# The gate's rows formed per sequence inside the middle pass, with both Newton roots on VectorE

## The chip, the cores and the metric

The kernel runs on one core of a Trainium2 chip. The metric is the device time of one launch in microseconds (us). The engines are TensorE (PE; PEld is its weight load), VectorE (DVE), ScalarE (ACT), GpSimd (POOL) and SyncE (SP), which issues DMAs. Each engine runs its own instructions in order and waits on semaphores for the others.

## The reference

x has 4096 rows of 256 numbers. Six layers are added to it one after the other, each on the layer norm of x: self-attention; an attention over 64 context rows a sequence, with quantised weights; eight pairs of linear maps; a mixture of 8 experts; a masked attention; a quantised feed-forward pair. The change concerns the gate of the fourth layer:

```python
xn = rmsnorm(xf, gate_norm_w, 1e-6)              # xf: layer norm of x, 4096 x 256
xq = act_quant(rmsnorm(xn, gate_in_norm_w, 1e-8))  # per row: round(x * 127 / max|x|) ...
wq = weight_quant(gate_w)                        # 8 x 256, three values
gate_logits = xq @ wq.T
probs = softmax(gate_logits); topw, topi = top_k(probs, 2)
# one expert: its first C = 512 rows of xf (rms-normed), up, silu gate, down, times the row's weight
```

## The kernel before

x stays on the chip as X, 128 partitions by 32 tiles of 256 (four tiles a sequence, eight sequences, besides spare tiles). The stages follow one another, each a block of programs for the five engines: `self_attention`, `middle` (layers 2 and 3), `experts` (layer 4: a block for the gate, the routing and the experts' weights, then a block for the experts), `masked_attention`, `quantised_pair`.

`middle` loops over the sequences, unrolled, with B + 1 iterations. For each sequence TensorE turns the attention weights (`turn_weights`), turns the map's second weights (`turn_w2`, four jobs), computes the next sequence's scores, turns the normalised rows of the sequence before (`f_rows`, L1160), computes `values` (L1209), `outputs` of the sequence before (L1260), `pair` 0 and 1 (L1236: the product of the two maps), `turn_back` (L1273), `rows` of a later sequence and `turn_pair`. The order is written out by hand in each engine's loop, and again in `in_order`, which gives each job one of eight PSUM banks in turn; `take(bank)` waits until the engine that read the bank's last content has released it. ScalarE copies every turned block out of PSUM (L1427 `weights_out`, L1434 `w2_out`, L1411 `f_rows_out`, L1442 `pair_turned`, L1404 `rows_turned_out`, L1454 `wT_turned`, L1461 `outputs_out`) and normalises rows (L1397 `f_normalise`, L1389 `normalise`). VectorE takes the maxima of the scores (L1528), adds the values to X, computes the statistics and the inverse root of the next layer norm (L102 to L135) and adds the outputs (L1564, `add_outputs`), behind which it takes the statistics of the finished rows (L71). GpSimd has eight copies of 8 columns in this stage.

The gate's block begins when `middle` has ended. VectorE aggregates the statistics of all 32 tiles, computes roots by Newton steps (`rsqrt`, L122), forms v = (X - mean) * norm1 and a = v * norm2 in a rolled loop over the sequences (L1985, L1990), takes peaks (L1993), and ScalarE sums the squares of v (L1827). After two more roots VectorE quantises the rows (L2028, L2031), TensorE turns them (L1882), ScalarE copies them (L1834) and TensorE multiplies by the gate's weights (L1888). GpSimd forms u, the rows that the experts get (L1806). From L2041 on VectorE computes the softmax, the two best experts and each row's slot (L2099), after which GpSimd scatters u by slots into the DRAM tensor expert_in, 64 indirect DMAs (L1814); expert_in has first been filled with zeros (L1774). Beside this the experts' weights are loaded (L1783, L1784), summed, rounded to three values and turned.

`masked_attention` handles 32 tiles, four to a sequence; its loops over the first seven sequences are unrolled on GpSimd, TensorE, ScalarE and VectorE (`for b in range(B - 1)`).

Of the kernel before, what the change touches and what calls it, by code (L numbers as in the profile page):

```python
# [1027 lines left out]
def middle(core, context, w_q, b_q, w_k, b_k, w_v, b_v, w_1, b_1, w_2, b_2):  # L1028
# [3 lines left out]
    nc, X, ps, ident = core.nc, core.X, core.ps, core.ident  # L1032
# [4 lines left out]
    BANKS, EARLY = 8, 6  # L1037
    with ExitStack() as ctx:
# [32 lines left out]

        loaded, b_loaded = lasting("loaded"), lasting("b_loaded")
# [15 lines left out]
        early = ["c0", "c1", "cols", "wq", "k0", "k1"] + [f"v{i}" for i in range(B // 2)] + ["wk0", "wk1", "bk"]  # L1088
# [3 lines left out]
        for b in range(B + 1):  # L1092
            if b < B:
                in_order += [("pT", b), ("w2T", b, 0), ("w2T", b, 1)]
            if b + 1 < B:
                in_order += [("scores", b + 1)]
            if b < B:
                in_order += [("w2T", b, 2), ("w2T", b, 3)]
            if b:
                in_order += [("f_rows", b - 1, 0), ("f_rows", b - 1, 1)]  # L1100
            if b < B:
                in_order += [("av", b, 0), ("av", b, 1)]
            if b:
# [3 lines left out]
            if b:  # L1107
                in_order += [("back", b - 1, 0), ("back", b - 1, 1)]
# [4 lines left out]
            if b < B:  # L1113
                in_order += [("wT", b)]
        bank_of = {job: n % BANKS for n, job in enumerate(in_order)}

        with nc.Block() as block:
            @block.sync
            def _(sp):
# [6 lines left out]
                sp.dma_start(bv_row[:], row_of(b_v)).then_inc(loaded, 16)  # L1126
                sp.dma_start(b1_rows[:], b_1.rearrange("g (c p) -> (g c) p", p=P)).then_inc(b_loaded, 16)
# [10 lines left out]
                sp.wait_ge(b_loaded, 16 * 2)  # L1138

            @block.gpsimd  # L1140
            def _(pool):
                pool.wait_ge(cols_out, 1)
                pool.sem_inc(cols_out, -1)
                for g in range(B):
                    if g >= 2:
                        pool.wait_ge(b1_used, 1)
                        pool.sem_inc(b1_used, -1)
                    nc.gpsimd.tensor_copy(w1[:, g % 2, :, D:D + 1], b1_col[:, g * FC:(g + 1) * FC].unsqueeze(2)).then_inc(b1_set, 1)
# [4 lines left out]
            def _(pe):  # L1153
# [122 lines left out]

                for bank in range(BANKS):
                    pe.sem_inc(free[bank], 1)
                pe.wait_ge(loaded, 16 * 9)
                for c in range(DC):  # L1280
                    take(early_bank[f"c{c}"])
                    for t in range(CT):
# [6 lines left out]
                                    ident[0:B * DC, 0:B * DC]).then_inc(cols_full, 1)  # L1289
                over.turn(pe, peak[:])  # L1290
# [38 lines left out]
                last.then_inc(pre_full, 1)  # L1329
                for c in range(DC):  # L1330
# [9 lines left out]
                for b in range(B + 1):  # L1340
                    if b < B:
                        turn_weights(b)
                        turn_w2(b, 0)
                        turn_w2(b, 1)
                    if b + 1 < B:
# [4 lines left out]
                    if b:  # L1350
                        for c in range(DC):
                            f_rows(b - 1, c)
                    if b < B:
                        values(b, 0)
                        values(b, 1)
                    if b:
# [4 lines left out]
                    if b:  # L1361
# [7 lines left out]
                    if b < B:  # L1369
                        turn_pair(b)  # L1370
                for bank in range(BANKS):
# [3 lines left out]
            def _(act):  # L1375
# [87 lines left out]

                act.wait_ge(loaded, 16 * 9)
# [24 lines left out]
                for b in range(B + 1):  # L1489
                    if b < B:  # L1490
                        weights_out(b)
                        w2_out(b, 0)
                        w2_out(b, 1)
                    if b < B:
                        w2_out(b, 2)
                        w2_out(b, 3)
                    if b:
                        for c in range(DC):
                            f_rows_out(b - 1, c)
                    if b + 1 < B:  # L1500
                        powers(b + 1)
                    if b:
# [11 lines left out]
                    if b + 3 < B:  # L1514
                        normalise(b + 3)

            @block.vector
            def _(dve):
# [4 lines left out]
                def less_maximum(bank):  # L1523
# [8 lines left out]
                    dve.drain().then_inc(less_top, 1)  # L1532

# [35 lines left out]

                for b in range(2):  # L1570
# [4 lines left out]
                dve.drain().then_inc(over.ready, 1)  # L1575
# [1709 lines left out]
```

## Time and profile before

| | us |
|---|---|
| median of 3 runs | 2373.59 (2372.21 to 2380.17) |
| the profiled execution's own time | 2368.86 |
| its span, first to last instruction | 2367.1 |
| mean granted TensorE clock | 0.853 of full speed |
| busy: TensorE / VectorE / ScalarE / GpSimd | 1715.8 / 1550.3 / 1394.6 / 788.3 |

Times of instructions are counted from the start of the span. Busy time leaves out waits, register and semaphore instructions. The stages begin, by their first instructions, at about 1097.8 (middle), 1370.3 (gate, routing and weights), 1609.8 (experts), 1823.0 (masked attention) and 2196 us (quantised pair). A number in brackets behind an instruction is the time for which its engine was idle before it, with what ended that.

### The profile page before, as it was taken

The numbers are of one execution on the slowest core, as the hardware profiler recorded it, in microseconds if no ns is written. First come the engines' busy times: TensorE is split into PE (matmuls) and PEld (weight loads), VectorE is DVE, ScalarE is ACT, GpSimd is POOL, SyncE is SP. The second block draws the span as 40 slices with busy tenths as digits, with TensorE's granted clock in tenths as the row PEclk, the third lists the DMA queues.
The fourth block names the chain that finished last, engine by engine and source line by source line (L and its number), as shares of the span: only waits on it lengthen the run. The fifth ranks groups of instructions, "written<-read, shape, count | busy, mean of one in ns | idle before, by whom it ended". The sixth has DMA issues, their size and how long they took to land. (4 is left out here: it accounts for less than half of the span.)

```text
span 2367.1 us, 42843 instructions
## 1 busy us (share of the span) xinstructions
PE 1715.8 (72%) x13321; PEld 1084.2 (46%) x13338; DVE 1550.3 (65%) x3111; ACT 1394.6 (59%) x2215; POOL 788.3 (33%) x749
## 2 busy tenths in 40 slices
PE   3789998989999898985888802122443788888577
PEld 1455555555555555553666601121222355555323
DVE  6877777777777777775233386744774675755775
ACT  3889888898979898991444412443553332323745
POOL 0534545454545455450000050470001444443000
PEclk9999999999999999996789955555766787878699
DMA  5222222222222222222122111332102201111001
GB/s 180 61 53 62 59 55 64 61 53 62 62 50 64 59 64 53 64 46 97 36 72 72 36 76 53 122 109 89 54 27 70 81 25 30 23 32 18 1 10 63
DMA packets 173822, 140.04 MB, mean 59 GB/s; under 512 B 83794, under 2 KB 155399, under 8 KB 173366
## 3 DMA queue, kind: packets, MB, share of 16 engines
q1 hardware_dynamic: 166710, 122.78, 19.4%
q0 software_dynamic: 6912, 14.71, 2.7%
q8 instruction: 111, 1.82, 0.3%
q14 instruction: 89, 0.73, 0.1%
HBM read 61.92 MB, written 20.97 MB: 35 GB/s over the span
## 5 line engine op out<-in xcount | busy, mean ns | idle before, releaser
L577 ACT ACTIVATE a_p_hi<-ps,a_probs_up,a_s_scale 128x512 f16<-128x512 f32 x512 | 397.7, 777 | 54.9 <-ACTq L575 54.1
L689 DVE TENSOR_REDUCE a_top<-ps 128x2 f32<-128x1024 f32 x256 | 313.1, 1223 | 132.6 <-DVEq L688 132.6
L578 ACT ACTIVATE a_probs<-ps,a_probs_up,a_s_scale 128x512 f32<-128x512 f32 x512 | 398.5, 778 | 0.0
L917 POOL TENSOR_TENSOR a_p_lo<-a_probs,a_p_hi 128x1024 f16<-128x1024 f32 x128 | 277.8, 2170 | 210.4 <-POOLq L916 169.1
L905 POOL TENSOR_TENSOR a_ops<-a_ident_down,a_top 64x256 f16<-64x256 f32 x256 | 158.9, 621 | 340.8 <-POOLq L900 332.3
L698 DVE TENSOR_TENSOR a_p_lo<-a_probs,a_p_hi 128x1024 f16<-128x1024 f32 x128 | 182.7, 1427 | 41.2 <-DVEq L697 41.2
L441 PE MATMUL ps<-a_ops 128*128 128x512 f16 x512 | 195.8, 382 | 17.7 <-PEq L439 17.6
L460 PE MATMUL ps<-a_v_hi,a_p_hi 128*128 128x65 f16 x2048 | 205.6, 197 | 2.1 <-PEq L455 2.0
L463 PE MATMUL ps<-a_v_lo,a_p_hi 128*128 128x64 f16 x2048 | 205.6, 195 | 0.0
L464 PE MATMUL ps<-a_v_hi,a_p_lo 128*128 128x65 f16 x2048 | 205.5, 196 | 0.0
L460 PEld LDWEIGHTS ps<-a_v_hi,a_p_hi 128*128 128x128 f16 x2048 | 191.2, 99 | 23.0 <-issue 11.1
L463 PEld LDWEIGHTS ps<-a_v_lo,a_p_hi 128*128 128x128 f16 x2048 | 190.6, 100 | 13.1 <-issue 1.4
L442 PE MATMUL ps<-a_ops 128*128 128x512 f16 x512 | 196.0, 383 | 0.0
L464 PEld LDWEIGHTS ps<-a_v_hi,a_p_lo 128*128 128x128 f16 x2048 | 190.6, 99 | 0.0
L427 PE MATMUL ps<-a_qk,a_qd 128*128 128x512 f16 x512 | 152.7, 380 | 46.1 <-PEq L425 45.9
L414 PE MATMUL ps<-a_wp,a_oT 128*128 128x256 f32 x512 | 128.7, 396 | 1.1 <-PEq L370 1.1
L2498 POOL TENSOR_TENSOR x_s<-x_s,x_top 128x1024 f32<-128x1024 f32 x32 | 60.8, 1899 | 156.2 <-POOLq L2497 106.4
L1814 POOL DMA_INDIRECT expert_in<-g_u,m_slot x64 | 79.2, 1237 | 100.9 <-POOLq L1811 81.7
L671 DVE SCALAR_TENSOR_TENSOR a_qk<-ps,a_qk 128x512 f16<-128x512 f32 x128 | 88.5, 691 | 34.9 <-DVEq L670 34.9
L385 PE MATMUL ps<-a_xnT,a_wq 128*128 128x512 f16 x384 | 94.5, 382 | 20.7 <-PEq L370 20.7
L414 PEld LDWEIGHTS ps<-a_wp,a_oT 128*128 128x128 f32 x512 | 94.8, 195 | 12.2 <-issue 1.3
L427 PEld LDWEIGHTS ps<-a_qk,a_qd 128*128 128x128 f16 x512 | 46.0, 97 | 117.1 <-issue 82.7
(487 smaller groups left out, 3767.3 us busy)
## 6 DMA issues: line engine op xcount, KB each, us to landing
a_ops<-a_qk SPq DMA_DIRECT2D x384, 128.0 KB, 2.3
f_w<-in_L_ffn_W_dram SPq DMA_DIRECT2D x16, 1024.0 KB, 7.6
a_qd<-a_qk SPq DMA_DIRECT2D x128, 64.0 KB, 2.2
g_a<-in_L_attn_gp_w_dram SPq DMA_DIRECT2D x8, 1024.0 KB
X<-in_x_dram SPq DMA_DIRECT2D x8, 512.0 KB, 9.9
expert_in<-g_w SPq DMA_DIRECT2D x8, 512.0 KB
g_a<-in_L_attn_dp_w_dram SPq DMA_DIRECT2D x8, 512.0 KB
e_x_in<-expert_in SPq DMA_DIRECT2D x8, 512.0 KB, 4.3
```

The lines of the kernel that those rows point to most:

```text
L414: last = nc.tensor.matmul(ps[:, JOB + bank, 0:D], oT[:, c, t * P:(t + 1) * P], wp[:, c, :], start=(c % (HC // 2) == 0), stop=(c % (HC // 2 ...
L427: last = nc.tensor.matmul(ps[:, ROW + j % 2, :], qd[:, s, j, :], qk[:, s, K_HI, :], start=True, stop=True)
L441: nc.tensor.matmul(ps[:, st_bank(n), :], ops[:, s, i, A_K, keys], ops[:, s, i, A_Q, :], start=True, stop=False)
L442: nc.tensor.matmul(ps[:, st_bank(n), :], ops[:, s, i, B_K, keys], ops[:, s, i, B_Q, :], start=False, stop=True).then_inc(st_full, 1)
L460: first = nc.tensor.matmul(ps[:, AV, at:at + HD + 1], hi, v_hi[:, k, h, :], start=(k == 0), stop=False)
L463: nc.tensor.matmul(ps[:, AV, at:at + HD], hi, v_lo[:, k, h, :], start=False, stop=False)
L464: last = nc.tensor.matmul(ps[:, AV, at:at + HD + 1], lo, v_hi[:, k, h, :], start=False, stop=(k == KT - 1))
L577: nc.scalar.activation(p_hi[:, h % 2, k, :], scores, ACT.Exp, bias=probs_up[:], scale=s_scale[:])
L578: nc.scalar.activation(probs[:, h % 2, k, :], scores, ACT.Exp, bias=probs_up[:], scale=s_scale[:]).then_inc(st_taken, 1)
L689: nc.vector.tensor_reduce(top[:, c % 2, 2 * pair:2 * pair + 2], ps[:, ROW:ROW + 2, :], AX.X, ALU.max).then_inc(row_taken, 1)
L698: nc.vector.tensor_tensor(p_lo[:, h % 2, 0:2, :], probs[:, h % 2, 0:2, :], p_hi[:, h % 2, 0:2, :], ALU.subtract).then_inc(p_made, 1)
L917: nc.gpsimd.tensor_tensor(p_lo[:, h % 2, 2:KT, :], probs[:, h % 2, 2:KT, :], p_hi[:, h % 2, 2:KT, :], ALU.subtract).then_inc(p_made_pool, 1)
```

## The change

The gate's block keeps only what follows L2041. All that stood before is moved into `middle`: its loop gets B + GATE_STEPS = 13 iterations instead of B + 1 = 9, and a sequence's gate is worked on in five steps, each an iteration behind the other. `f_rows` moves ahead of `scores` on TensorE and `f_rows_out` ahead of two of the `w2_out` on ScalarE. u is formed by ScalarE instead of GpSimd, and ScalarE instead of VectorE does the rounding. The buffers `gate.u` and `gate.logits` live from `middle` to the experts; `a` has three slots of one sequence. The experts' weights no longer wait for the gate (`w_used` is given at once). In `masked_attention` the four unrolled loops become loops of the engines with b in a register.

The diff, cut to its core:

```diff
-        for b in range(B + 1):
+        for b in range(B + GATE_STEPS):          # in_order, and on TensorE, ScalarE, VectorE
             if b < B:
                 in_order += [("pT", b), ("w2T", b, 0), ("w2T", b, 1)]
+            if 1 <= b <= B:
+                in_order += [("f_rows", b - 1, 0), ("f_rows", b - 1, 1)]
+            if 0 <= b - GATES < B:
+                in_order += [("gates", b - GATES)]
             if b + 1 < B:
                 in_order += [("scores", b + 1)]
...
+            if 0 <= b - QUANTISE < B:
+                in_order += [("gate_rows", b - QUANTISE)]
+    NORMS, ROWS, SQUARES, QUANTISE, GATES = 1, 2, 3, 4, 5
...
+                sp.dma_start(gw[:], gate_w).then_inc(gate_loaded, 16)
+                sp.dma_start(norm1[:], row_of(gate_norm)).then_inc(gate_loaded, 16)
+                sp.dma_start(norm2[:], row_of(gate_in_norm)).then_inc(gate_loaded, 16)
...
+                def gate_rows(b):      # TensorE, last in an iteration
+                    for t in range(TT):
+                        for c in range(DC):
+                            last = nc.tensor.transpose(ps16(bank)[:, at:at + P], g_r[:, t, c * P:(c + 1) * P], ident16[:])
+                def gates(b):          # TensorE, between f_rows and scores
+                    for t in range(TT):
+                        for c in range(DC):
+                            last = nc.tensor.matmul(ps[:, bank, t * E:(t + 1) * E], g_rT[:, t, c, :], gwT[:, c, :], ...)
...
+                def experts_rows(b):   # ScalarE
+                    act.wait_ge(u_ready, 1)
+                    for t in range(TT):
+                        nc.scalar.activation(gate.u[:, n, :], X[:, n, :], ACT.Identity, scale=u_factor[:, t:t + 1], bias=u_shift[:, t:t + 1])
+                    act.wait_ge(v_made, 1)
+                    for t in range(TT):
+                        nc.scalar.activation(g_junk[:, t * D:(t + 1) * D], g_v[:, t, :], ACT.Square, accum_out=squares[:, t:t + 1])
+                    act.drain().then_inc(squared, 1)
+                def quantise(b):       # ScalarE
+                    act.wait_ge(per_made, 1)
+                    for t in range(TT):
+                        nc.scalar.activation(a[:, t, :], a[:, t, :], ACT.Identity, scale=per[:, b % 2, t:t + 1], bias=up[:])
+                    act.drain()
+                    nc.scalar.activation(g_r, a, ACT.Identity, bias=minus_up[:])
+                def gate_rows_out(b):  # ScalarE: 128 x 1024 bf16 out of PSUM
...
                     if b < B:
                         pair_turned(b, 0)
+                    if 0 <= b - QUANTISE < B:
+                        quantise(b - QUANTISE)
+                    if b < B:
                         pair_turned(b, 1)
...
                     if b + 3 < B:
                         normalise(b + 3)
+                    if 0 <= b - QUANTISE < B:
+                        gate_rows_out(b - QUANTISE)
+                    if 0 <= b - ROWS < B:
+                        experts_rows(b - ROWS)
...
+                def gate_norms(b):     # VectorE: 4 bn_aggr, 3 small, 2 paired, seed (2 paired + 1), 3 Newton steps of 3
+                def gate_values(b):    # 2 paired, 1 small -> u_ready; v: 4 rows -> v_made; a: 128 x 1024; peaks
+                def gate_squares(b):   # wait squared; 3 small, seed, 3 Newton steps of 3
+                def gate_steps(b):     # 6 small -> per_made
+                def gate_logits(b):    # wait gates_full; 1 small, releases the bank
...
                     if b < B:
                         add_values(b)
                         f_statistics(b)
-                    if b:
+                    if 0 <= b - GATES < B:
+                        gate_logits(b - GATES)
+                    if 0 <= b - SQUARES < B:
+                        gate_squares(b - SQUARES)
+                    if 0 <= b - ROWS < B:
+                        gate_values(b - ROWS)
+                    if 1 <= b <= B:
                         add_outputs(b - 1)
+                    if 0 <= b - NORMS < B:
+                        gate_norms(b - NORMS)
+                    if 0 <= b - SQUARES < B:
+                        gate_steps(b - SQUARES)
```

In `experts`, on VectorE (TensorE, ScalarE and GpSimd lose their parts of the gate in the same way), and in `masked_attention`:

```diff
                     nc.vector.memset(zeros, 0.0).then_inc(zeros_made, 1)
                     nc.vector.memset(ones_col[:], 1.0)
                     nc.vector.memset(ones[:], 1.0)
-                    row_moments(core, dve)
-                    ...                       # L1943 to L2039: roots, v, a, peaks, quantised rows, logits
+                    dve.sem_inc(w_used, 2)
+                    dve.wait_ge(made, 1)
+                    dve.sem_inc(made, -1)
+                    nc.vector.tensor_copy(number[:], counting[:])
+                    dve.drain()
+                    nc.vector.tensor_scalar(base[:], number[:], float(ROOM), -float(ROWS), ALU.mult, ALU.add)
                     nc.vector.tensor_reduce(top[:], logits[:], AX.X, ALU.max)
...
-                for b in range(B - 1):
+                with pool.Fori(0, B - 1) as b:      # the same on TensorE, ScalarE and VectorE
```

## Rows read from the trace of the kernel before

**Rows 1.** Busy by stage: stretch, length, PE, PEld, DVE, ACT, POOL (instructions), clock, DMA share, GB/s.
```profile
1097.80:1370.30 272.50, 221.83 (x1028) 164.28 (x1028) 98.75 (x375) 114.23 (x266) 1.51 (x8) 0.85 0.20 68
1370.30:1483.30 113.00, 15.79 (x132) 11.71 (x132) 84.14 (x199) 21.85 (x72) 34.67 (x21) 0.50 0.19 68
```
**Rows 2.** Timeline of the gate's block and its end: start, us, engine, instruction, idle before.
```profile
1370.59 0.91 DVE L1938 MEMSET g_w<- 128x1024 f32 x1 [0.55 <-PEq L1117]
...
1483.25 0.42 DVE L2041 TENSOR_REDUCE g_top<-g_logits 128x32 f32<-128x256 f32 x1
...
1503.27 0.16 DVE L2097 TENSOR_SCALAR m_slot<-m_share 128x8 uint32<-128x8 f32 x1
...
1504.56 1.53 POOL L1814 DMA_INDIRECT expert_in<-g_u,m_slot  x1 [81.70 <-POOLq L1811]
...
1609.86 0.06 DVE L2388 MEMSET e_minus_round<- 128x1 f32 x1 [34.67 <-PEq L1766]
```
**Rows 3.** Timeline of one sequence of the middle pass, ScalarE and TensorE.
```profile
1225.76 0.38 ACT L1442 ACTIVATE f_both<-ps 128x256 f32<-128x256 f32 x1 [3.82 <-ACTq L1441]
...
1231.20 2.08 ACT L1389 ACTIVATE c_xn<-X,c_shift,c_ln_rstd 128x256 f32<-128x256 f32 x4
...
1233.47 0.59 ACT L1427 ACTIVATE c_probsT<-ps 64x512 f32<-64x512 f32 x1 [0.19 <-ACTq L1426]
...
1238.23 0.60 ACT L1411 ACTIVATE f_xnT<-ps 128x512 f32<-128x512 f32 x1 [0.20 <-ACTq L1410]
...
1239.40 5.97 PE L1260 MATMUL ps<-f_xnT,f_wT 128*128 128x512 f32 x8 [3.05 <-PEq L1156]
...
1249.57 3.65 PE L1236 MATMUL ps<-f_w,f_w2T 128*128 128x257 f32 x16
...
1253.34 0.38 ACT L1442 ACTIVATE f_both<-ps 128x256 f32<-128x256 f32 x1 [3.82 <-ACTq L1441]
```
**Rows 4.** Busy time and clock of two stretches of the same sequence.
```profile
1233.47:1245.37 11.90, 8.56 (x23) 4.50 (x22) 5.90 (x27) 5.92 (x16) 0.00 (x0) 0.71 0.04 11
1245.37:1253.10 7.73, 7.73 (x42) 6.74 (x41) 2.69 (x6) 1.22 (x3) 0.00 (x0) 1.00 0.00 0
```
**Rows 5.** The line L1427, once a sequence: durations in ns, first and last start.
```profile
L1427 ACT ACTIVATE c_probsT<-ps x8: 590/590/590, 1151.6 to 1336.6; 64x512 f32<-64x512 f32 x8
```
**Rows 6.** Busy time and DMA share behind the start of the gate's block.
```profile
1380.00:1390.00 10.00, 0.35 (x2) 0.28 (x2) 8.58 (x22) 0.66 (x3) 5.94 (x3) 0.50 0.37 147
```
**Rows 7.** Prices of operations like the moved ones: timeline, and one line.
```profile
1240.21 0.16 DVE L131 TENSOR_TENSOR f_ln_tmp<-f_ln_rstd 128x4 f32<-128x4 f32 x1
...
1240.44 0.16 DVE L133 TENSOR_TENSOR f_ln_tmp<-f_ln_tmp,f_ln_half 128x4 f32<-128x4 f32 x1
...
1426.65 1.66 DVE L1985 SCALAR_TENSOR_TENSOR g_v<-X,mean_var,g_norm 128x256 f32<-128x256 f32 x4
...
1428.51 1.23 DVE L1990 TENSOR_TENSOR g_a<-g_v,g_norm 128x1024 f32 x1 [0.20 <-issue]
...
1486.68 1.06 ACT L1844 ACTIVATE g_junk<-g_a 128x1024 bf16<-128x1024 f32 x1
...
L1827 ACT ACTIVATE g_junk<-g_v x32: 398/401/417, 1389.3 to 1438.5; 128x256 bf16<-128x256 f32 x32
```
**Rows 8.** VectorE's last work in the middle pass.
```profile
1368.64 1.41 DVE L71 BATCH_NORM_STATS2 row_stats<-X 128x6 f32<-128x256 f32 x4
```
**Rows 9.** Transposes with and without register addresses, and a loop's branch on TensorE.
```profile
1463.46 1.21 PE L1882 MATMUL ps<-ident,g_r 128*128 128x128 bf16 x8 [0.57 <-PEq L1878]
...
1510.70 1.86 PE L1911 MATMUL ps<-ident,g_w 128*128 128x128 bf16 x16 [12.92 <-PEq L1908]
...
L2330 PEldq COMPARE_BRANCH  x6: 83/215/215, 1669.2 to 1783.4; - x6
```
**Rows 10.** Masked attention from the first to the last tile's turned weights, 31 tiles.
```profile
1883.60:2188.60 305.00, 251.25 (x1157) 174.27 (x1156) 193.57 (x413) 90.09 (x121) 136.85 (x107) 0.81 0.15 28
```

More of the change, by code:

```diff
@@ L1289, in _ @@
                                     ident[0:B * DC, 0:B * DC]).then_inc(cols_full, 1)
+                pe.wait_ge(gw_part, 1)
+                pe.sem_inc(gw_part, -1)
+                take(early_bank["gw"])
+                nc.tensor.matmul(ps[:, early_bank["gw"], 0:1], ones[:], gw_sum[:], start=True, stop=True).then_inc(gw_total, 1)
                 over.turn(pe, peak[:])
@@ L1329, in _ @@
                 last.then_inc(pre_full, 1)
+                pe.wait_ge(gw_round, 1)
+                pe.sem_inc(gw_round, -1)
+                take(early_bank["gwT"])
+                for c in range(DC):
+                    last = nc.tensor.transpose(ps[:, early_bank["gwT"], c * E:(c + 1) * E], gw[:, c * P:(c + 1) * P], ident[0:E, 0:E])
+                last.then_inc(gw_turned, 1)
                 for c in range(DC):
@@ L1338, in _ @@
                 pe.sem_inc(v_made, -1)
-                for b in range(B + 1):
+                for b in range(B + GATE_STEPS):
                     if b < B:
@@ L1344, in _ @@
                         turn_w2(b, 1)
+                    if 1 <= b <= B:
+                        for c in range(DC):
+                            f_rows(b - 1, c)
+                    if 0 <= b - GATES < B:
+                        gates(b - GATES)
                     if b + 1 < B:
@@ L1488, in _ @@
                 normalise(2)
-                for b in range(B + 1):
+                for b in range(B + GATE_STEPS):
                     if b < B:
@@ L1493, in _ @@
                         w2_out(b, 1)
+                    if 1 <= b <= B:
+                        for c in range(DC):
+                            f_rows_out(b - 1, c)
                     if b < B:
@@ L1496, in _ @@
                         w2_out(b, 3)
[L1497 to L1499 removed]
                     if b + 1 < B:
                         powers(b + 1)
[L1502 removed]
+                    if 1 <= b <= B:
                         for m in range(DC):
@@ new lines, in gate_logits @@
+                def gate_logits(b):
+                    bank, seq = bank_of["gates", b], slice(b * TT, (b + 1) * TT)
+                    dve.wait_ge(gates_full, 1)
+                    dve.sem_inc(gates_full, -1)
+                    nc.vector.scalar_tensor_tensor(out=gate.logits[:, seq, :], in0=ps[:, bank, 0:TT * E].rearrange("p (t e) -> p t e", e=E),
+                                                   scalar=gw_mean[:], in1=g_step[:, seq].unsqueeze(2).broadcast_to([P, TT, E]),
+                                                   op0=ALU.mult, op1=ALU.mult).then_inc(free[bank], 1)
@@ L1568, in add_outputs @@
                         row_statistics(core, b * TT + t)
+                nc.vector.memset(ones[:], 1.0)
+                nc.vector.memset(gw_sum[:], 0.0)
+                nc.vector.memset(up[:], ROUND)
+                nc.vector.memset(minus_up[:], -ROUND)
                 for b in range(2):
@@ L2653, in _ @@
                 ahead.turn(pe)
-                for b in range(B - 1):
+                with pe.Fori(0, B - 1) as b:
                     sequence(b, more=True)
@@ L2718, in _ @@
                 power(0)
-                for b in range(B - 1):
+                with act.Fori(0, B - 1) as b:
                     sequence(more=True)
@@ L2808, in _ @@
                 maximum(0, 1)
-                for b in range(B - 1):
+                with dve.Fori(0, B - 1) as b:
                     sequence(b, more=True)
```

350 lines of the change are left out of this document (167 added, 183 removed).

## The prediction

> **What bounds the kernel now.** I read the busy time by stage first. The stage from 1370.30 to 1483.30 us, the gate, is the one that the change takes out: 113.0 us in which VectorE is busy 84.14, ScalarE 21.85 and TensorE 15.79 [rows 1]. It is a serial chain. It ends when VectorE takes the row maxima of the logits (L2041) at 1483.25 [rows 2]; everything that the change keeps begins there. From L2041 to the last slot is 20.3 us, then GpSimd, idle for 81.70 us before it, scatters for 105 us, and the next block starts at 1609.9 [rows 2]. The expert weights, rounded beside the scatter, do not set that end: VectorE, which rounds them, has been idle for 34.67 us when it comes [rows 2]. So a us taken out ahead of L2041 is a us of the whole, as long as the filling of the inbox with zeros, the other thing that the scatter waits for, stays ahead.
>
> The second view is one sequence of the middle pass, in order of time. The work that the gate is moved into is not slack. From the copy of one sequence's second pair product (L1442, 1225.76) to TensorE's outputs (L1260, 1239.40) ScalarE works without a gap: it copies, normalises (L1389 and its like), copies again (L1427, L1434, L1411), and L1260 waits 3.05 us for the last of these copies [rows 3]. After that wait the granted clock is low: 0.71 over the stretch with L1260, 1.00 over the one behind it [rows 4]. So ScalarE's burst, 13.6 us, and TensorE's stretch from L1260 to the end of L1236, 13.8 us, add up with the hand-overs to the local period, 27.6 us from one L1442 to the next; the mean period, by L1427, is 185.0/7 = 26.4 us [rows 5]. VectorE is busy only 98.75 of the stage's 272.5 us [rows 1].
>
> **Part 1: the gate's stage goes.** Ahead of L2041 there remain the memset of zeros, two small ones, the wait for GpSimd's constants and two copies of 8 columns: from 1370.59 about 2.0 us instead of 112.7 [rows 2]. That is -110.6 us. GpSimd's own u rows ended long before the scatter and save nothing by themselves. Bounds: -111 (nothing in the way) to -104. The latter is the inbox: its zeros are written until the window 1380 to 1390 (DMA share 0.37) and were started at about 1371.6, so they land some 13 us after the stage begins [rows 6]; slots are now made at 2.0 + 20.3 = 22.3 us, 9 us later. The first two experts' weights are now queued right behind the zeros, and their load may lengthen that; I leave 7 us for it in the range and nothing in the sum.
>
> **Part 2: what a sequence's gate costs VectorE.** A small operation with its drain starts every 0.24 us (1240.21 to 1240.44) [rows 7]. `gate_norms`, `gate_squares`, `gate_steps` and `gate_logits` have 15 + 14 + 6 + 1 such steps, 8.7 us, and the aggregates and paired operations 0.6. `gate_values` has three small ones, four rows in 1.66, a 1024-wide product of 1.23 and a maximum of the same length: 5.0 us [rows 7]. Together 14.4 us a sequence, both roots being here; with the 98.75/8 = 12.3 us of now VectorE is busy some 27 of a period of 30 at the worst. It stays behind TensorE only by its order: `f_normed` comes ahead of the new work, `less_maximum` comes 10 us after it. I cost this at nothing in the steady state. If the cover fails, the bank of `gates` (released by VectorE's `gate_logits`) is the one that `pair` 0 takes, 8 banks later: VectorE releases it about 5.8 us after `values`, about when L1260 ends.
>
> **Part 3: what it costs ScalarE, which is on the path.** `experts_rows` stands at the end of an iteration, ahead of the next `weights_out`: four scaled rows as in L1389, 2.08 us, and four squares at 0.40 us with their drain, 1.9; `gate_rows_out` reads 1024 columns, 1.06 by the nearest row, 1.25 with its drain [rows 3, 7]. `quantise` (2.08 + 1.06 + drains = 3.4 us) stands between the two pair products' copies, where ScalarE waits 3.82 us anyway [rows 3]: nothing. In the other direction the new order puts `f_rows_out` ahead of two `w2_out`, so that L1260 need not wait for these: 2 x 0.80 = -1.6 us. By sequence: iteration 1: -1.6; iterations 2 and 3: +4.0 - 1.6 = +2.4 each; iterations 4 to 7: +5.2 - 1.6 = +3.6 each. Sum +17.6. TensorE's own additions (eight transposes of 128 columns, eight products of 8) are some 1.3 us a sequence and lie in the time that it waits for ScalarE; that wait grows to some 7 us, and with it the chance that more of L1260 and the pair product behind it run at the low clock: at most 2 us a sequence, of which I take 0.7, or +5. Steady state: +23, between +5 (ScalarE's additions half hidden) and +40 (the bank of part 2 and the clock both in full).
>
> **Part 4: head and tail of the middle pass.** Head: three loads, two small TensorE jobs, and the rounding of the gate's weights ahead of four batches of statistics: +1.4 us, 0 to 3. Tail: four more iterations, in which nothing covers the chain of sequence 7. From the end of its statistics, 1368.64 + 1.41 = 1370.05 [rows 8]: norms 4.2, steps of sequence 5 1.5, logits and squares of 6 3.8, values of 7 5.0, steps of 6 1.5, logits and squares of 7 3.8, steps of 7 1.5: 21.3. `quantise` of 7 is done at 25.6 (ScalarE is first held by sequence 6 until 22.3), the transposes at 27.1, the copy at 28.4, the products at 29.3, the logits at 29.7. +30 us, 26 to 36.
>
> **Part 5: the masked attention's loop.** The diff also rolls it up on four engines. What was a constant becomes a register. Eight transposes with a register address take 1.21 us, sixteen without one 1.86: 151 against 116 ns, +35 ns each [rows 9]. TensorE has ten such products a tile, VectorE's two or three lie behind waits at perhaps 0.1 us together: 0.45 x 28 tiles = 12.6. A TensorE loop branch takes 0.215 us [rows 9], seven of them 1.5. Upper end 14, lower end 0 if all is hidden in the 9.8 us that a tile takes (305.0/31) [rows 10]; TensorE and waits for it make most of a tile, so I take rather more than half, +8. The Trainium skill ("Advanced Engine Details and Errata", Control Flow Timing) gives a compare-and-branch about 108 ns. By it the seven would be 0.8 us instead of 1.5; the row is twice that on TensorE.
>
> **Sum:** -110.6 + 23 + 1.4 + 30 + 8 = -48 us. The profiled execution took 2368.86 us (span 2367.1); the median of the three runs is 2373.59, 4.7 above. -48 from the median gives 2325, from the profiled one 2321. I say 2324.
>
> **The rivals.**
> A: *the middle pass absorbs it.* ScalarE's new work meets gaps after all and the rolled loop is free: steady +8, loop 0, giving -71: 2303. For it: TensorE is the busiest engine there (221.83 of 272.5) [rows 1] and ScalarE less than half busy. Against: the burst ahead of L1260 has no gap [rows 3]. Chance 0.2.
> B: *VectorE becomes the bound of the middle pass.* The two roots hold `add_outputs` or the gates' bank, and each of seven periods grows by 4 us more: -20, 2354. For it: 27 busy us with in-order waits in a period of 30. Against: by my order of events each release comes 0 to 2 us ahead of its use. Chance 0.2.
> C: *slower: the jump back of the rolled loop.* If each jump has to fetch its code anew, the seven jumps of the slowest engine stand on the path. It decides from (48 + 7)/7 = 7.9 us a jump. Against it: the branches of the expert loops, six on TensorE, show 0.215 us [rows 9]; the gain of part 1 is there anyway. At 9 us a jump it would be -48 + 63 = +15: 2389. Chance 0.04. The Trainium skill ("Advanced Engine Details and Errata", ISA Cache) says that the instruction cache has two lines of 256 instructions, more on TensorE. By this rule only a body above 512 instructions would fetch on each turn, and no row here counts a body.
> D: *the stage does not shrink as said:* the scatter is held by the zeros or the weights queued behind them by over 30 us, with the middle pass lengthened all the same: about 2360 to 2373. Chance 0.03.
> My forecast: 0.53.
>
> **How the numbers follow.** Forecast's own range is 2310 to 2338 (loop 0 to 14, tail and steady state by half their bounds). To hold 8 in 10 it has to reach over most of A and of B: 2299 to 2353. 0.3% is 7 us, about what this kernel's runs (2372.21 to 2380.17) can tell from no change. Faster: the forecast, A, B and half of D, with a little taken off for what I have not seen: 0.94. Within 0.3%: 0.02. Slower: 0.04.
>
> **What would show it.** In the changed profile: the block of the experts' weights should last about 129 us from its first memset to the next block instead of 239; GpSimd's scatter should begin 23 us after it; the middle pass should last about 327 us instead of 272.5, 30 of them behind sequence 7's statistics; the distance of L1427's successors should be under 27 us in the first sequences and about 30 from the fifth on, with L1260's successor waiting for ScalarE's copies and not for VectorE; a tile of masked attention should take 10.1 us instead of 9.8. The prediction is wrong if less_maximum or add_outputs is late in the middle pass (B), if the first matmul behind a jump waits (C), or if the scatter starts later than 25 us (D).

## The result, and the profile after

The changed kernel takes 2303.27 us, the median of four runs (2302.21 to 2308.77), beside 2372.9 us of the kernel before: ratio 0.9715, 95% interval 0.9674 to 0.9757, so 58 to 77 us less. Measured once more, on the chip of the first experiments, it took 2306.23 us beside 2370.48, ratio 0.9726 (0.9701 to 0.9751), so 64 us less. The prediction was 2324, 49 us less; the time lies in its range, and it is faster as said. But the number is that of rival A (2303), and neither of A's two reasons holds: the middle pass did not absorb the gate, and the rolled loop was not free, it gave 16.9 us. And 2303 lies outside the forecast's own range, 2310 to 2338; only the wider range, which was stretched over A, holds it.

First the stages of the changed kernel, from the profiled execution (2308.77 us, span 2307.0). The stretches are the middle pass, the block of the experts' weights, the middle pass from the first to the last weights_out (L1508, seven periods), and masked attention from its first to its last tile (31 tiles); the columns are as in [rows 1].

```profile
1102.10:1437.20 335.10, 247.85 (x1160) 182.27 (x1160) 188.57 (x803) 177.60 (x410) 1.83 (x11) 0.78 0.17 56
1437.20:1567.30 130.10, 25.97 (x210) 23.51 (x210) 67.04 (x205) 49.02 (x57) 81.87 (x66) 0.55 0.47 162
1158.50:1366.80 208.30, 179.87 (x871) 137.56 (x870) 117.96 (x497) 118.58 (x288) 1.21 (x6) 0.85 0.18 61
1839.30:2127.10 287.80, 225.16 (x1157) 157.86 (x1156) 193.16 (x413) 90.12 (x121) 138.25 (x108) 0.89 0.16 29
```

The same two stretches of the kernel before, the seven periods and the 31 tiles:

```profile
1151.60:1336.60 185.00, 165.33 (x817) 127.56 (x817) 63.54 (x240) 87.47 (x211) 1.18 (x6) 0.88 0.21 69
1882.50:2187.20 304.70, 251.96 (x1157) 174.44 (x1156) 193.40 (x413) 89.93 (x121) 137.78 (x107) 0.80 0.15 28
```

The middle pass grew from 272.8 to 335.1 us (+62.3), the experts' first block shrank from 239.3 to 130.1 (-109.2), and the masked attention's tiles, which the gate never touches, shrank from 304.7 to 287.8 (-16.9). The self-attention ahead of it all, which the change does not touch, ended 4.3 us later (in a second profile of the changed kernel 2.1 us earlier, so this is spread). These four make -59.5 of the -60.1 between the two spans; the medians lie 69.6 us apart, and the other 9.5 us are spread between runs that no profile splits up. In the last row TensorE executes the same 1157 products as before, but is busy 27 us less, at a clock of 0.89 instead of 0.80. That is the surprise.

The end of the middle pass and the scatter answer to [rows 2] and [rows 8], from the timeline:

```profile
1405.42 1.41 DVE L71 BATCH_NORM_STATS2 row_stats<-X 128x6 f32<-128x256 f32 x4
...
1434.83 0.36 PE L1341 MATMUL ps<-gate_gwT,gate_rT 128*128 128x8 bf16 x8 [1.48 <-PEq L1202]
1435.35 0.25 DVE L1743 SCALAR_TENSOR_TENSOR gate_logits<-ps,gate_gw_mean,gate_step 128x32 f32<-128x32 f32 x1 [5.73 <-DVEq L1742]
...
1437.16 0.91 DVE L2114 MEMSET g_w<- 128x1024 f32 x1 [1.56 <-PEq L1159]
...
1438.44 0.41 DVE L2123 TENSOR_REDUCE g_top<-gate_logits 128x32 f32<-128x256 f32 x1
...
1459.75 1.24 POOL L2030 DMA_INDIRECT expert_in<-gate_u,m_slot  x1 [21.97 <-issue]
```

From the end of sequence 7's statistics (1406.83) to the next block's memset there are 30.3 us, before 0.5: the tail costs 29.8, and 30 was said. The scatter starts 22.6 us into the block (23 was said), and the block lasts 130.1 us (129 was said).

### The profile page after: what moved, and what is told of

Its sections match the earlier page's. It is cut to its first block and busy times, and to the rows that moved or that the text cites. A ratio compares the mean times of both kernels' runs of the same rounds, so it can differ in the third digit from the quotient of the medians.

```text
span 2307.0 us, 43352 instructions
## 1 busy us (share of the span) xinstructions
PE 1705.8 (74%) x13321; PEld 1076.1 (47%) x13338; DVE 1558.2 (68%) x3345; ACT 1437.8 (62%) x2287; POOL 756.4 (33%) x732
## 5 line engine op out<-in xcount | busy, mean ns | idle before, releaser
L441 PE MATMUL ps<-a_ops 128*128 128x512 f16 x512 | 197.8, 386 | 17.8 <-PEq L439 17.7
L460 PEld LDWEIGHTS ps<-a_v_hi,a_p_hi 128*128 128x128 f16 x2048 | 191.8, 100 | 23.3 <-issue 12.0
L385 PE MATMUL ps<-a_xnT,a_wq 128*128 128x512 f16 x384 | 94.5, 382 | 20.6 <-PEq L370 20.6
L385 PE MATMUL ps<-a_xnT,a_wk 128*128 128x512 f16 x384 | 93.9, 381 | 5.5 <-PEq L370 5.4
```

The source lines that it names most:

```text
L385: last = nc.tensor.matmul(ps[:, JOB + bank, :], w[:, i, d, c * P:(c + 1) * P], xnT[:, j, d, :], start=(n == d == 0), stop=(n == len(PARTS) ...
L441: nc.tensor.matmul(ps[:, st_bank(n), :], ops[:, s, i, A_K, keys], ops[:, s, i, A_Q, :], start=True, stop=False)
L460: first = nc.tensor.matmul(ps[:, AV, at:at + HD + 1], hi, v_hi[:, k, h, :], start=(k == 0), stop=False)
```

## The experiments

Four questions: is it the loop that shortens masked attention, by which engine, and how; does VectorE or ScalarE set the middle pass's period; what is the new order worth; and can the middle pass be had cheaper. "The 31 tiles" and "seven periods" are the two stretches above. Eleven changed kernels and the changed kernel itself were run.

**The loop alone, on the kernel before.**

```
-                for b in range(B - 1):
+                with pe.Fori(0, B - 1) as b:      # and so for pool, act, dve
```

> The kernel before with only the masked attention's loop over the sequences rolled up on its four engines; nothing else of the change. It prices part 5 alone. The masked attention took 288.2 us for 31 tiles in the changed kernel instead of 305.0, at a granted clock of 0.90 instead of 0.81. Theory R (the roll itself does it): 288 us for 31 tiles here too (9.3 us a tile), the whole 15 to 17 us shorter than before. Rival L (what stands ahead of it does it: the gate's stage is gone, the code or the tiles lie elsewhere, or it differs from run to run): 300 to 315 us for 31 tiles, and by my own prices (35 ns for each TensorE product with a register address, 0.215 us a branch) the whole 0 to 14 us longer.

Measured: ratio to before 0.9938 (0.9915 to 0.9962), 2354.39 us beside 2370.48. The 31 tiles took 288.2 us at a clock of 0.89, and seven periods of the middle pass 183.2, as before. The loop alone gives the gain of the masked attention. Theory R holds; my price for it had the wrong sign.

**The mirror: the changed kernel with the loop written out.**

> The changed kernel with the masked attention's loop written out again on all four engines; the gate stays in the middle pass. Theory R (the roll gives the 17 us): 305 us for 31 tiles at a clock near 0.81, and the whole 15 to 17 us longer than the changed kernel, about 2318 to 2320 us beside its 2303. Rival L (the move of the gate gives it): 288 us for 31 tiles at 0.90, the whole within 5 us of the changed kernel. My prediction's price (rolled is 8 us dearer) would make it 8 us shorter than the changed kernel, about 2295.

Measured: 2314.95 us beside 2306.23 of the changed kernel on the same chip; ratio to before 0.9767 (0.9734 to 0.9801). The 31 tiles took 293.9 us, between the two. The single tiles, read from one x_pT (ScalarE's copy of a tile's turned attention weights) to the next, show why: of the seven sequences one ran at the full clock throughout its long tile (12.9 us), two fell once (17.3), the other four as in the kernel before (19.3 to 19.7). Not all of the 12.9 is the clock: in that tile VectorE makes x_o (the tile's output, for which TensorE waits) 1.3 us behind x_pT, in the others 2.9 to 3.5 us behind it, and the tile two places ahead of it took 11.6 us at a clock of 0.85 instead of 9.97. Written out, the same code falls into one pattern or the other; its runs spread over 20 us (2305.58 to 2325.85), those of the rolled kernel over 7.

**The changed kernel once more.**

> The changed kernel itself once more, on the same chip as the others, so that they can be set against it, and a second profile of it. If the 288.2 us for 31 tiles of masked attention belong to the kernel, they stand within 2 us again; if they vary by chance with the clock, they may be anywhere from 288 to 305.

Measured: 2306.23 us, ratio 0.9726 (0.9701 to 0.9751). The 31 tiles took 288.0 us, so they belong to the kernel (from the sixth tile to the thirtieth it is 225.6 and 225.9 us in the two profiles of the changed kernel and 245.5 in that of the kernel before; the first tiles vary by some us whatever is changed). The seven periods took 214.2 us and not 208.3:

```profile
1150.40:1364.60 214.20, 185.93 (x871) 141.34 (x870) 117.97 (x497) 118.57 (x288) 1.20 (x6) 0.82 0.18 60
```

The difference lies in the first two periods (26.3 and 32.0 us instead of 28.2 and 24.1); the other five agree within 0.2. Three other profiles with this order show the second form (214.2, 214.1, 214.1), so it is the usual one, and I go by it below.

**TensorE's loop rolled alone; then the other three without it; then VectorE's alone.** All on the kernel before, with the one line above.

> The kernel before with the masked attention's loop rolled up on TensorE alone. So far: unrolled, the 31 tiles took 304.7 us (all four engines written out, before) and 293.8 (written out, in the changed kernel), rolled on all four 287.8 to 288.2 in three profiles. A sequence's long fourth tile shows why: rolled, the granted clock falls once in it (17.3 us, and 4.33 for the next tile); unrolled it falls a second time behind a short wait of TensorE (19.3 us, and 5.9). Theory P (it is TensorE's own instruction order and timing in its loop that keep the second fall away): 288 us here. Theory O (it is when the other engines deliver): 300 to 305 us. A loop on TensorE alone should show in any case tiles at the full clock of 10.11 and 5.85 us instead of 9.97 and 5.67, if the register addresses cost what I gave them.

> The mirror of the run with TensorE alone: the kernel before with the loop rolled up on ScalarE, VectorE and GpSimd, TensorE's written out. Theory P: 300 to 305 us for the 31 tiles, tiles at the full clock of 9.97 and 5.67 us. Theory O: 288 us.

> The kernel before with the masked attention's loop rolled up on VectorE alone. Rolled on ScalarE, VectorE and GpSimd it gave 284.2 us for the 31 tiles, on TensorE alone 300.1, on none 304.7. If it is VectorE (its register addresses move when it frees the scores and hands over x_o): 284 to 290 us and the whole about 15 us shorter, with one tile of each sequence at 10.11 us instead of 9.97. If it is GpSimd or ScalarE: 300 to 305 us and the whole unchanged.

Measured: TensorE alone 1.0005 (0.9994 to 1.0016), the 31 tiles 300.1 us. The other three 0.9941 (0.9923 to 0.9959), 284.2 us. VectorE alone 0.9921 (0.9896 to 0.9947), 288.4 us. So VectorE's loop is enough, and TensorE's does not do it. Theory P, TensorE's own order, falls; theory O holds. No run rolls ScalarE's or GpSimd's loop alone, or all but VectorE's. The forms are not clean everywhere: with TensorE's loop alone two of the seven long tiles (17.1 us) fall once as well, and with the other three rolled three of seven take 14.7 us, each with a tile of 11.6 us two places ahead of it; with VectorE's alone one of seven does.

What happens is seen in single tiles. Four tiles of one sequence, from x_pT to x_pT, in the kernel before; then in the changed one; then with VectorE's loop alone; then with TensorE's alone. The long tile is the first row of each:

```profile
1986.40:2005.60 19.20, 13.25 (x49) 9.49 (x50) 10.18 (x18) 3.80 (x6) 10.66 (x9) 0.63 0.32 51
2005.60:2011.60 6.00, 5.86 (x28) 3.60 (x27) 2.51 (x3) 1.98 (x3) 0.00 (x0) 0.75 0.14 16
2011.60:2021.90 10.30, 9.20 (x44) 6.07 (x44) 9.29 (x19) 3.83 (x5) 3.91 (x3) 1.00 0.00 1
2021.90:2027.60 5.70, 5.53 (x33) 4.16 (x32) 4.54 (x20) 2.27 (x4) 3.90 (x4) 1.00 0.03 7
```

```profile
1943.40:1960.80 17.40, 10.34 (x49) 7.26 (x50) 10.27 (x18) 3.83 (x6) 10.35 (x9) 0.80 0.25 43
1960.80:1965.10 4.30, 4.23 (x28) 3.04 (x26) 2.30 (x2) 1.97 (x2) 0.50 (x1) 1.00 0.63 69
1965.10:1975.20 10.10, 9.14 (x44) 6.09 (x44) 9.10 (x18) 3.84 (x5) 3.14 (x2) 1.00 0.00 0
1975.20:1981.10 5.90, 5.63 (x34) 4.17 (x32) 4.80 (x21) 2.24 (x3) 4.14 (x4) 1.00 0.00 0
```

```profile
1958.10:1975.50 17.40, 10.61 (x49) 7.43 (x50) 10.28 (x18) 3.82 (x7) 10.33 (x9) 0.80 0.19 45
1975.50:1979.80 4.30, 4.18 (x28) 3.10 (x26) 2.35 (x2) 1.95 (x2) 0.50 (x1) 1.00 0.42 66
```

```profile
1984.40:2004.00 19.60, 13.27 (x49) 9.55 (x50) 10.10 (x18) 3.84 (x7) 10.60 (x9) 0.63 0.29 50
2004.00:2009.70 5.70, 5.56 (x28) 3.53 (x26) 2.51 (x3) 1.98 (x3) 0.00 (x0) 0.78 0.12 11
```

The same 49 products take 13.3 us in one and 10.3 in the other, because of the clock. Finer stretches of the long tile, before and after:

```profile
1988.00:1994.00 6.00, 4.11 (x7) 2.07 (x8) 4.03 (x9) 1.33 (x2) 3.91 (x3) 0.51 0.25 44
1995.00:1998.00 3.00, 2.57 (x22) 2.29 (x20) 2.56 (x6) 0.30 (x1) 1.16 (x1) 1.00 0.12 18
1999.00:2008.00 9.00, 7.41 (x21) 4.62 (x20) 0.85 (x2) 2.84 (x4) 3.91 (x4) 0.50 0.42 58
```

```profile
1945.00:1951.00 6.00, 3.75 (x6) 1.82 (x7) 4.38 (x9) 1.34 (x2) 3.92 (x3) 0.50 0.21 41
1952.00:1955.00 3.00, 2.48 (x22) 2.21 (x20) 2.82 (x5) 0.40 (x1) 0.69 (x1) 1.00 0.21 26
1955.00:1964.00 9.00, 6.31 (x39) 4.68 (x40) 2.53 (x5) 3.04 (x5) 5.23 (x5) 1.00 0.43 56
```

In both the clock falls to half (1.2 of 2.4 GHz) within TensorE's wait for x_o (3.65 us before, 3.90 after), and comes back. In the kernel before it falls a second time, between the second and the third of these rows, and stays low for all 9 us of the third; in the changed one TensorE has gaps there too (6.31 of 9 us busy), and the clock stays. The sequence saves 19.2 + 6.0 - 17.4 - 4.3 = 3.5 us, and six such make 21. The first sequence does not have it (26.2 us instead of 24.1 for these two tiles), and the rest of the difference to 16.9 is the price of the addresses and of the first tiles. The register addresses do cost something, and it can be read where both run at the full clock: from one x_pT to the next 9.97 us becomes 10.11 with VectorE rolled, 5.67 becomes 5.85 with TensorE rolled. That is 0.32 us a sequence in these two tiles, some 2 us in all. The other two tiles can't be read for it.

**A filler in TensorE's wait.** If the fall of the clock is the loss, work that fills the wait should prevent it.

```
                         turn_weights(t)
+                        if t == 3 and more:
+                            for n in range(24):
+                                nc.tensor.transpose(ps[:, OT, n % DC * P:(n % DC + 1) * P], ident[:], ident[:])
                         if t:
                             turn_outputs()
```

> The changed kernel with 24 more TensorE transposes of the identity a sequence in masked attention, ahead of the wait for x_o in the fourth tile, into the part of PSUM that is written next; nothing reads them. TensorE waits 3.9 us there, and behind that wait its clock falls from 1.00 to 0.50 for some 6 us. Theory K (what costs the time in the long tile is the clock that falls behind TensorE's wait): at the full clock the 24 take some 2.8 us and fit into the wait, the clock stays at 1.00, the long tile takes 13 us instead of 17.3, the 31 tiles some 260 us instead of 288, the whole about 28 us shorter. Rival W (the waits themselves are the time, the clock only a sign of them): the 31 tiles unchanged at 288 or up to 7 us longer.

Measured: ratio 0.9722 (0.9705 to 0.9738), 2305.65 us, no gain over the changed kernel. The 31 tiles took 283.0 us instead of 288.0, but this is not the filler's: the last six long tiles, each with the tile behind it, take 130.0 us in all, beside 129.8 and 130.0 in the two profiles of the changed kernel. What differs is the first sequence, and the run with the rows u on GpSimd (below), which has no filler, is as short (282.0 us). Two long tiles of this run, one of each kind:

```profile
1863.54:1879.10 15.56, 10.80 (x72) 8.59 (x71) 10.27 (x18) 3.93 (x7) 10.05 (x9) 1.00 0.18 51
1899.44:1916.75 17.31, 12.62 (x72) 10.06 (x71) 10.27 (x18) 3.93 (x6) 10.82 (x9) 0.82 0.24 55
```

The wait for x_o is 1.3 to 1.5 us instead of 3.9, and the clock stays at 1.00 through it in all seven sequences. In two of the seven it stays through the whole long tile (15.4 and 15.6 us), which is then 1.8 us shorter than the 17.3 with a single fall; not 4.4, since x_o comes no sooner than without the filler (3.2 to 3.4 us behind x_pT). In the other five the clock falls later, 11 to 14 us into the tile, where TensorE has shorter waits (16.0 to 17.3 us). Theory K is right that the fall costs time and wrong about the size: in the long tile it costs 1.8 us, the rest of the difference to 12.9 is when x_o comes; and where the first wait is filled, the clock can still fall in shorter ones behind it.

**VectorE or ScalarE in the middle pass.** First one Newton step fewer in each root.

```
-                    for _ in range(3):
+                    for _ in range(2):
```

> The changed kernel with two Newton steps instead of three in each of the gate's two roots (this changes the computation: the roots come out a little less exact). It takes 2 x 3 small operations of 0.24 us, 1.45 us a sequence, off VectorE and off nothing else. My prediction (VectorE is covered in the steady state and on the path in the tail): the seven periods unchanged beyond their own spread (208 to 214 us), the tail, three roots long, some 2.2 us shorter (two roots of sequence 7 and one of sequence 6), the whole -2. Rival B (VectorE bounds the middle pass): seven periods some 10 us shorter.

Measured: seven periods 214.1 us beside 214.2; ratio 0.9703 (0.9684 to 0.9723), too wide to tell -2 from nothing. VectorE is 5 us less busy in these periods (113.00 instead of 117.97) and nothing follows it. Rival B falls. But the tail, where I expected 2.2 us, is shorter by 0.3 to 0.5 only (29.95 us beside 30.24 to 30.42 in the other profiles with this tail). In it ScalarE takes over: it starts to quantise sequence 6 right behind its own squares, 0.8 us after VectorE's factors are there.

Then the rows u on GpSimd.

```
+                    if b >= 2:                        # sequence b - 2, behind the copy of b_1's column
+                        for x, y, op in ((X, mean_var[:, seq, 0], ALU.subtract), (gate.u, u_factor[:], ALU.mult)):
+                            nc.gpsimd.tensor_tensor(gate.u[:, seq, :], x[:, seq, :], y..., op)
 def experts_rows(b):
-                    for t in range(TT):
-                        nc.scalar.activation(gate.u[:, n, :], X[:, n, :], ACT.Identity, scale=u_factor..., bias=u_shift...)
```

> The changed kernel with the experts' rows u (four ScalarE operations, 2.08 us a sequence) made by GpSimd in two operations of 1024, some 4.2 us, in the time that it is idle in the middle pass. Theory S (ScalarE's burst, with TensorE's stretch behind it, sets the middle pass's period, and its new work is on the path one for one): six periods 2.1 us shorter, the middle pass 12 us shorter (323 instead of 335), the whole about 2291. Rival V (VectorE bounds it): no change, or a us or two longer where GpSimd's operations slow VectorE's down. Rival T (TensorE's own work at its low clock bounds it): less than 5 us.

Measured: seven periods 204.5 us instead of 214.2, -9.7 where -12 was expected: theory S holds, ScalarE's burst is on the path, and nearly one for one: the seven periods held the rows of five sequences, 10.4 us of ScalarE's work (the -12 counts a sixth, behind the last weights_out). Of the 9.7, 4.3 us are TensorE's busy time (181.62 instead of 185.93) and the rest its waits. But the whole is 2306.64 us, the same as the changed kernel's. What follows the last weights_out grew from 70.4 to 82.0 us, 8.2 of these 11.6 us ahead of the last statistics and 3.4 in the tail, for VectorE, whose line for gate_v this is, is slowed down while GpSimd works:

```profile
L1710 DVE SCALAR_TENSOR_TENSOR gate_v<-X,mean_var,gate_norm x32: 472/1300/2123, 1223.2 to 1420.6; 128x256 f32<-128x256 f32 x32
```

Its median is 1300 ns; without GpSimd beside it 477 (475 to 485). Four of these a sequence are hidden while TensorE is the later one, and not behind the last weights_out.

**The order of f_rows.**

```
                        w2_out(b, 1)
-                    if 1 <= b <= B:
-                        for c in range(DC):
-                            f_rows_out(b - 1, c)
                    if b < B:
                        w2_out(b, 2)
                        w2_out(b, 3)
+                    if 1 <= b <= B:
+                        for c in range(DC):
+                            f_rows_out(b - 1, c)      # TensorE and the banks alike
```

> The changed kernel with f_rows and f_rows_out at their old place in the middle pass (behind the last two w2T jobs, on TensorE, on ScalarE and in the order of the banks). My prediction costed the new place at -1.6 us for each of seven sequences (L1306 need not wait for two copies more), so this should be 11 us longer. Rival C (the clock): in the new place TensorE stands at f_rows (L1206) for ScalarE's f_xn up to 2.2 us a sequence, ahead of the scores, and its clock falls there, 14 us ahead of the outputs and not right at them; undoing it lets TensorE begin the scores earlier: the seven periods 200 to 208 us instead of 214, the whole 5 to 14 us shorter.

Measured: ratio 0.9791 (0.9766 to 0.9815), 2322.91 us; seven periods 229.5. So the new order is worth 15.3 us there, where I gave it 9.6 (six of seven times 1.6). The sum came out near, but not for my reason, 1.6 us in each sequence: the first five periods change by 0.8 us in all, 148.7 instead of 147.9. Rival C falls: with the old order TensorE waits 21.9 us in all at the outputs (L1308; 1.1 us at the same line of the changed kernel, L1306) and is busy no longer than with the new one (184.05 us, 185.93), and nearly all of the 15.3 lies in the last two periods (41.8 and 38.9 us instead of 34.6 and 31.7).

**The gates' products later.**

```
                    if b < B:
                        turn_w2(b, 2)
                        turn_w2(b, 3)
+                    if 0 <= b - GATES < B:
+                        gates(b - GATES)               # was ahead of scores; the banks alike
```

> The changed kernel with the products of the gates moved two places back on TensorE (behind scores and the last two w2T jobs, ahead of the values), so that TensorE does not stand at them (5.1 us in three of seven sequences) for ScalarE's copy of the gate's rows. Theory C (TensorE's waits early in the iteration cost both themselves and the clock behind them): seven periods 5 to 12 us shorter than 214, the whole as much. Rival S (the period is ScalarE's burst and TensorE only waits elsewhere then): the wait moves to the values or the outputs, the periods within 3 us of 214.

Measured: ratio 0.9664 (0.9641 to 0.9687), 2294.75 us, the best of all. Seven periods take 205.3 us; the first five are those of the changed kernel within 0.1 us, the last two 29.4 and 28.0 instead of 34.6 and 31.7, and these are the ones in which gates are formed. The largest of TensorE's waits in the seven periods, first the changed kernel and then this one:

```profile
PE ps L1206 <- PEq L1202: 11.6, 6, 2.2
PE ps L1341 <- PEq L1202: 5.1, 3, 3.2
PE ps L1255 <- PEq L1202: 3.8, 2, 1.9
```

```profile
PE ps L1208 <- PEq L1204: 11.4, 6, 2.2
PE ps L1257 <- PEq L1204: 4.7, 4, 1.9
PE ps L1343 <- PEq L1204: 3.8, 2, 3.0
```

The waits hardly shrink: those at the gates by 1.3 us (L1341, now L1343), while those at the values grow by 0.9 (L1255, now L1257), and what the periods hold beside TensorE's busy time goes from 28.3 to 26.9 us. But TensorE is busy 178.36 us instead of 185.93 for the same 871 products, at a clock of 0.85 instead of 0.82. That is 7.6 of the 8.9 us: what is won is mostly the clock.

**Both, with GpSimd kept out of the tail.**

> The changed kernel with the gates' products two places later on TensorE, and the rows u of sequences 0 to 5 on GpSimd, those of 6 and 7 left on ScalarE, where the tail has room. Each by itself: later gates, seven periods 205.3 us, the whole 2294.75; all u on GpSimd, seven periods 204.5, but the tail 11.6 us longer, as VectorE's gate_v takes 1.30 us instead of 0.42 to 0.48 beside GpSimd. If the two gains add and the tail stays at 70 us: seven periods 195, the whole about 2285. If both remove the same wait: periods 204, the whole 2294 again.

Measured: ratio 0.9683 (0.9668 to 0.9697), 2297.08 us. The seven periods add up as hoped (196.0 us), but 76.7 us follow them instead of 70.4. They are lost ahead of the last statistics (46.2 us from the last weights_out to the last of them, instead of 39.6), where add_outputs stands behind a gate_v of 0.78 us on average; the tail itself is 30 us. Nothing is gained over the later gates alone.

## Why the prediction was right, and where it was not

The account, in us, by the profile after (in brackets the second form, which four of five profiles show); part 3's +23 is split as its sum by iterations has it:

| step | said | measured |
|---|---|---|
| part 1, the gate's stage | -110.6 | -109.2 |
| part 4, head of the middle pass | +1.4 | +2.6 (+0.9) |
| part 3, seven periods (iterations 0 to 6) | +18.2 | +23.3 (+29.2) |
| part 3, iteration 7, up to the last statistics | +4.3 | +6.5 |
| part 4, tail | +30 | +29.8 |
| part 5, the loop | +8 | -16.9 |

- **Part 1** held: the block 130.1 us, the scatter at 22.6. The zeros and the weights did not hold it (D falls), and the first products behind the jumps show no stall (C falls: TensorE's loop alone changes nothing).
- **Part 2** held. VectorE's cover was there: with 5 us less on it the seven periods did not move.
- **Part 3** had the right mechanism, ScalarE's burst, and two sizes wrong. The clock was given 5 us. In the usual form TensorE is busy 20.6 us longer (185.93 beside 165.33). Of these the gate's own products in that stretch are 2.8, by the groups of instructions:

```profile
L1331 PE MATMUL ps<-ident,gate_r 128*128 128x128 bf16 x24 | 1.8, 219 | 0.0
L1341 PE MATMUL ps<-gate_gwT,gate_rT 128*128 128x8 bf16 x24 | 1.0, 167 | 5.1 <-PEq L1202 5.1
```

  The other 17.8 are, but for some 2 us of old products that the ends of the stretch take in, old products at the lower clock, most of all those of the values, the same 56 before and after:

```profile
L1209 PE MATMUL ps<-c_v,c_probsT 64*128 64x256 f32 x56 | 15.6, 424 | 1.5 <-PEq L1156 1.5
L1255 PE MATMUL ps<-c_v,c_probsT 64*128 64x256 f32 x56 | 23.1, 581 | 3.8 <-PEq L1202 3.8
```

  Waiting grew by 8.6. The waits are no longer where I said, at the outputs, but earlier, at f_rows, the gates and the values, so the clock falls earlier in the iteration and more work runs behind it. The seven periods are 26.3, 32.0, 27.9, 30.0, 31.8, 34.6 and 31.7 us: over 27 from the second on, earlier than I said. Iteration 7 grew by 6.5 instead of 4.3; how much of this is the change's is not settled, for the kernels with the old middle pass show it at 33.5 to 37.2 us, and 40.0 is the changed kernel's.
- **Part 4**, worked out operation by operation, was within 0.2 us in the tail. The run with fewer Newton steps shows how near VectorE and ScalarE lie there: neither chain alone sets those 30 us.
- **Part 5** is the step that failed: "TensorE and waits for it make most of a tile, so I take rather more than half, +8." It priced the instructions and took the clock as given. The instructions cost about 2 us where they can be read; with VectorE's loop rolled the clock no longer falls a second time in six of seven sequences, and that gives the rest, some 19. A tile takes 9.3 us on average, not the 10.1 that I gave as a sign. I had the clock's 0.81 in the row [rows 10] on which I priced the loop, and did not ask what a shift of some tenths of a us might do to it.

So it was luck that the range held: the loop was put 25 us too dear, and the middle pass 8 us too cheap (62.3 beside the 54.4 of parts 3 and 4; 12 us in its usual form): errors of opposite sign, of which the larger made the kernel 15 to 21 us better than said. Why VectorE's rolled loop, with 0.14 us more in a tile, keeps the clock from its second fall stays open: it was shown which engine's loop does it, not by which instruction. That x_o comes later is not enough: it is made 2.6 to 3.0 us behind x_pT in the long tiles of the kernel before and 3.2 to 3.3 in those of the changed one (the first sequence left out), but with TensorE's loop alone two long tiles with 2.7 us fall once, and in the mirror run one with 3.3 us falls twice.

## What to carry to other kernels

Work moved into a stage where two engines hand over to each other is paid twice: once for its duration on the one that is on the path, and again in the clock of TensorE, which waits for it; here the second part was the larger (17.8 us at the most, beside 2.8 us of new products and 8.6 us of waits). A row that is read at a granted clock well below 1.00 is no fixed price: ask which waits lie ahead of its falls, and put both forms into the range. In an in-order engine, an operation that waits for a slow partner belongs behind the work that is ready: one job moved two places, no work removed, gave another 0.5% (ratios 0.9664 and 0.9726; 2294.75 us and 2306.23, on two chips).

## What the runs showed of the hardware

- The clock of the same code takes one of a few discrete forms: the long tile lasts 12.9, 14.7, 17.3 or 19.3 us, and the first two periods of the middle pass 26.3 + 32.0 or 28.2 + 24.1 us, the latter with nothing changed in the kernel. Within one run the same seven sequences, written out, show three of the four. The Trainium skill ("TensorE: Matmul & The Clock Gate", Part 1) says that the throttled clock is the resting state and that activity releases it. The falls in TensorE's waits agree.
- Two tensor_tensor of 1024 columns on GpSimd (2.16 and 1.89 us) stretch VectorE's scalar_tensor_tensor of 256 columns, with two inputs in SBUF, from 0.48 to 1.30 us (median), up to 2.12. The Trainium skill ("GPSIMD Engine Reference", Key points) says that GpSimd shares its SBUF interfaces with VectorE and contends with instructions that have two SBUF inputs; the runs agree, and give it a size.
- 24 transposes of 128 columns in a wait of 3.9 us keep the clock at 1.00 through it in all seven sequences; in five of them it falls later in the tile, and the whole is no shorter.
